# Where a loop begins in VectorE's instruction pages, a fetch hint on TensorE's loop, and one expert group a step later

## The chip, the core and the metric

One core of a Trainium2 chip runs the whole program; the other seven are idle. The metric is the device time of one execution in microseconds (us). The kernel before was timed three times: 2798.35, 2799.54 and 2804.08 us, median 2799.54 us.

A core has five engines that run their own instruction streams and meet at semaphores: TensorE (PE in the rows; its weight loads are PEld), VectorE (DVE), ScalarE (ACT), GpSimd (POOL) and the DMA-issuing SyncE (SP). DMA engines move the data, and the engines' own instructions too.

## The reference

Three layers act on an image batch x of 32 x 64 x 16 x 16, which is 8192 tokens of 64 values:

```
x = x + conv3x3(groupnorm(x), circulant mix of the weight)
t = t + attention over 80000 edges (segment sums per node, exp of clipped scores)
t = t + moe(layernorm(t)):
    h = (x @ W_gat).reshape(M, 4 heads, 4 experts)
    e = leaky_relu(a_src[src] + a_dst[dst]);  softmax of e over the edges of each dst
    agg = segment_sum(h[src] * alpha, dst) + b_gat
    scores = mean over heads of layernorm(agg);  top-2 of 4 experts, softmax of the two
    out = sum over experts of g_e * (gelu(x @ W1[e] + b1[e]) @ W2[e] + b2[e])
```

The third layer has 262144 edges, of which those whose target lies within the 8192 tokens count. The change lies in the edge loop of this layer and in the stage after it.

## The kernel before

All engines' programs are written out by hand, with waits on counting semaphores. The stages in time: sort the attention's edges and convolve (to about 450 us), attend in 20 chunks while the third layer's edges are sorted (to about 1300 us), lay out the gating tables and run the first 14 of 16 expert groups (to about 1800 us), the **gating loop** (to 2653 us), and the **finish** (gates, top 2, experts 56 to 63, output; to the end).

**The gating loop.** The sorted edges are cut into chunks of 128 rows by 64 edges. How many chunks there are depends on the data (`n_all`, here 17, at most 32), so every engine that takes part runs a real loop over `it`, each pass with two halves `b = 0, 1` for chunk `it * 2 + b`, each half inside an `If` on `n_all`. VectorE's loop goes over `it = 1..16`, TensorE's over 1..15. With 17 chunks, passes 1 to 7 do two chunks, pass 8 does chunk 16 and then the last sums, and all later passes find every `If` false: they run only compares and branches.

In a half, GpSimd fetches 36 of the 64 source rows of a chunk with one indirect DMA each; the other 28 ("picks") come from TensorE, in 7 batches: `spread` (4 small matmuls) puts 4 columns of keys on all partitions, ScalarE's `all_keys` casts them, VectorE's `one_hot` compares them with 8 columns of numbers, `pick` runs 96 matmuls with the one-hot matrices as weights, and VectorE's `take_picked` picks the candidate. `pick` of a batch needs its `one_hot`; `one_hot` of batch m needs the `pick` of batch m - 2 (its buffer). Between the batches VectorE does `flags`, `maximum` and `weighted_sums` of the chunk before.

VectorE's half has 104 + 28 + 7 + 11 + 11 instructions as built, then a compare and a block of 27 for the last sums (`it * 2 + b == n_all`). The whole loop is 385 instructions as built, 8 of them branches to the very next instruction, which fall away. From the loop's first instruction counted, its branch targets that an empty pass visits are at 0 (head), 160, 187, 347 and 375; the last instruction, the back edge, is at 376. TensorE's loop body has 1447 rows as built, of which 1400 are matmuls with a weight load each, so about 2840 instructions.

**The finish.** The nodes are gated in 3 pieces, each in 4 parts, in the order `FINISH_ORDER` = (0,0) (0,1) (0,2) (0,3) (1,0) (1,1) (1,2) (2,0) (1,3) ... A part on VectorE ends in a semaphore for a ScalarE function (exp, sqrt, exp) that the next part waits for. The last 8 expert units (two groups of four) are put between: ScalarE does their gelus before its parts 1 and 2, and VectorE adds the groups' results (`expert_group(14)`, `(15)`) before its parts at places 2 and 3. TensorE runs the units one after the other; unit n's second matmuls need its gelu.

Of the kernel before, what the change touches and what calls it, by code (L numbers as in the profile page):

```python
# [56 lines left out]
G_CHUNKS = G_W // G_RUN  # L57
# [123 lines left out]
def build(nc, io, debug=None):  # L181
    with ExitStack() as ctx:
# [120 lines left out]
        first = r.at  # L303
# [184 lines left out]
        HS_FIRST, HS_EACH = 16 * G_RUN, 16 * (G_RUN - PICKS)  # L488

        EXPERTS_FIRST, EXPERTS_EARLY = 10, 14  # L490

        block = ctx.enter_context(nc.Block())

        def bc(ap, shape):
            return ap.to_broadcast(shape)
# [303 lines left out]
        def _(pe):  # L799
# [189 lines left out]
            def spread(it, b, m):  # L989

                if m == 0:
                    pe.wait_ge(pick_keys_set, it * 2 + (b - 1))
                pe.wait_ge(pick_all_set, chunk_count(it, b, BATCHES, m + 1))
                for k in range(BATCH):
                    last = nc.tensor.matmul(ps[turn_of(b, m)][:, k * P:(k + 1) * P], bc(pick_key[b][:, BATCH * m + k:BATCH * m + k + 1], [P, P]), ident16,  # L995
                                            start=True, stop=True)
                last.then_inc(pick_spread, 1)

            def pick(it, b, m):
                pe.wait_ge(pick_hot_set, chunk_count(it, b, BATCHES, m + 3))  # L1000
                pe.wait_ge(pick_taken, chunk_count(it, b, BATCHES, m + 1))
                for k in range(BATCH):
                    for t in range(K_TILES):
                        for n in range(SPLITS):
                            last = nc.tensor.matmul(ps[2 + turn_of(b, m)][:, k * PICK_W:(k + 1) * PICK_W], pick_hot[turn_of(b, m)][:, t, k * P:(k + 1) * P],  # L1005
                                                    h_split[n][:, t * PICK_W:(t + 1) * PICK_W],
                                                    start=t == 0 and n == 0, stop=t == K_TILES - 1 and n == SPLITS - 1)
                last.then_inc(picked, 1)
# [6 lines left out]
            with pe.If(n_all >= 3):  # L1015
                for m in range(2):
                    spread(1, 0, m)
            with pe.Fori(1, G_CHUNKS // 2) as it:
                for b in range(2):
                    with pe.If(it * 2 + b < n_all):  # L1020
                        for m in range(BATCHES - 2):
                            spread(it, b, m + 2)
                            pick(it, b, m)
                        for m in range(2):
                            pick(it, b, BATCHES - 2 + m)
                            with pe.If(it * 2 + (b + 1) < n_all):
                                spread(it + b, 1 - b, m)
# [59 lines left out]
        def _(act):  # L1087
# [135 lines left out]
            def gelu(n):  # L1223
                act.wait_ge(hid_done, n + 1)
                if n >= 2:
                    act.wait_ge(hid_used, n - 1)
                nc.scalar.activation(hid[n % 2], ps[4 + n % 2][:, :], ACT.Gelu, bias=b1[:, n % 4:n % 4 + 1]).then_inc(hid_set, 1)  # L1227
# [41 lines left out]
            def lay_out(n):  # L1269
                for k in range(G_PIECES[n][0] // 4, G_PIECES[n][1] // 4):  # L1270
                    act.wait_ge(out_turned, k + 1)
                    nc.scalar.copy(out_ch[:, 2 * k:2 * k + 2, :].rearrange("p j s -> p (j s)"), ps[k % 2][:, :]).then_inc(out_laid, 1)

            for at_, (n, part) in enumerate(FINISH_ORDER):
                if at_ in (1, 2):
                    for unit in range(4 * EXPERTS_EARLY + 4 * at_ - 4, 4 * EXPERTS_EARLY + 4 * at_):
                        gelu(unit)
                at = slice(2 * G_PIECES[n][0], 2 * G_PIECES[n][1])
                if part == 0:
                    act.wait_ge(node_exp_in, n + 1)  # L1280
                    for k in range(3):
                        nc.scalar.activation(n4[4 + k][:, at], n4[4 + k][:, at], ACT.Exp).then_inc(node_exp, 1)
                elif part == 1:
                    act.wait_ge(gate_root_in, n + 1)
                    nc.scalar.activation(ln_var[:, at], ln_var[:, at], ACT.Sqrt).then_inc(gate_root, 1)
                elif part == 2:
                    act.wait_ge(gate_exp_in, n + 1)
                    nc.scalar.activation(n4[8][:, at], n4[8][:, at], ACT.Exp).then_inc(gate_exp, 1)
                elif n >= 1:
                    lay_out(n - 1)  # L1290
# [4 lines left out]
        def _(dve):  # L1295
# [17 lines left out]
            def tt(o, a_, b_, op):  # L1313
                return V.tensor_tensor(o, a_, b_, op)  # L1314
# [429 lines left out]
            def expert_group(grp):  # L1744
                dve.wait_ge(hid_used, 4 * grp + 4)
                i0 = grp % 8 * 4
                for k in range(2):
                    ins = tt(exp_tile[:, grp // 8, i0 + 2 * k:i0 + 2 * k + 2], ps[6 + k][:, :].rearrange("p (i e c) -> p i e c", e=4, c=CH),
                             bc(b2.rearrange("p (e c) -> p e c", c=CH)[:, None], [P, 2, 4, CH]), ALU.add)
                ins.then_inc(exp_taken, 1)  # L1750
# [22 lines left out]
            def flags(it, b, back):  # L1773
                g_done[0] = 0
                dve.wait_ge(g_idx_in[b], it * 48 + (48 - 48 * back * b))
                link(it, b, back, tt(g_nst.rearrange("p (h j) -> p h j", j=G_COLS)[:, :, 1:], bc(g_didx[b][:, None, :], [P, G_HEADS, G_RUN]),
                                     bc(g_dprev[b][:, None, :], [P, G_HEADS, G_RUN]), ALU.is_equal))
                ts(g_cut, g_nst, BIG, ALU.mult, -BIG, ALU.add).then_inc(g_flags, 1)
# [58 lines left out]
            def one_hot(it, b, m):  # L1837
                dve.wait_ge(pick_all_set, chunk_count(it, b, BATCHES, m + 3))
                dve.wait_ge(picked, chunk_count(it, b, BATCHES, m + 1))
                for t in range(K_TILES):  # L1840
                    ins = ts(pick_hot[turn_of(b, m)][:, t], pick_all[turn_of(b, m)], node[:, t:t + 1], ALU.is_equal)
                ins.then_inc(pick_hot_set, 1)
# [11 lines left out]
            def picked_a_src(it, b):  # L1854
                rows_ = hs[b][:, G_RUN - PICKS:]
                prod_ = pick_prod[:, 0:PICKS * G_HF]
                pick_link(it, b, tt(prod_.rearrange("p (j f) -> p j f", f=G_HF), rows_[:, :, 0:G_HF], bc(att[:, 0:1, :], [P, PICKS, G_HF]), ALU.mult))
                pick_link(it, b, V.tensor_reduce(rows_[:, :, G_HF:], prod_.rearrange("p (j h k) -> p j h k", h=G_HEADS, k=G_EXP), AX_X, ALU.add))
# [12 lines left out]
                one_hot(1, 0, 1)  # L1871

            with dve.Fori(1, G_CHUNKS // 2 + 1) as it:
                for b in range(2):
                    with dve.If(it * 2 + b < n_all):
                        p_done[0] = 0
                        flags(it, 1 - b, 1)
                        for m in range(BATCHES - 2):
                            one_hot(it, b, m + 2)  # L1880
                            take_picked(it, b, m)
                            if m == 1:
                                maximum(it, 1 - b, 1)
                            if m == 2:
                                weighted_sums(it, 1 - b, 1)
                        for m in range(2):
                            dve.sem_inc(waits_carried, 1)
                            with dve.If(it * 2 + (b + 1) < n_all):
                                if m == 0:
                                    pick_keys(it + b, 1 - b)  # L1890
                                one_hot(it + b, 1 - b, m)
                            take_picked(it, b, BATCHES - 2 + m)
                        picked_a_src(it, b)
                        dve.sem_inc(waits_carried, 1)
                        assert p_done[0] == PICK_STEPS
                    with dve.If(it * 2 + b == n_all):
                        flags(it, 1 - b, 1)
                        maximum(it, 1 - b, 1)
                        weighted_sums(it, 1 - b, 1)
                        V.tensor_copy(row_tail, g_didx[1 - b][:, G_RUN - 1:G_RUN])  # L1900
                        dve.sem_inc(waits_carried, 1)
# [135 lines left out]
            step(ts(g_nodes.seed_f, g_nodes.carried, BIG, ALU.mult, -BIG, ALU.add))  # L2037
            parts = [finish(n, 2 * lo, 2 * hi) for n, (lo, hi) in enumerate(G_PIECES)]
            for at_, (n, _) in enumerate(FINISH_ORDER):
                if at_ in (2, 3):  # L2040
                    expert_group(EXPERTS_EARLY + at_ - 2)
                next(parts[n])

# [36 lines left out]
```

## Time and profile before

| | us |
|---|---|
| median of 3 runs | 2799.54 |
| the profiled execution | 2800.3 |
| its span | 2798.2 |
| VectorE busy | 1984.4 (71%) |
| GpSimd busy | 1758.9 (63%) |
| TensorE matmul busy | 1213.3 (43%) |
| ScalarE busy | 538.6 (19%) |

The span runs from the first to the last instruction of the program; 2.1 us of the execution lie around it. "Issue" in the rows is time in which an engine waited for nothing that the profile shows. Compares, branches and register operations are not counted as busy. DMA queues of the kind "instruction" carry the engines' programs.

### The profile page before, as it was taken

The page shows a single profiled execution, that of the slowest core. Times are in us where ns is not written, and L with a number is a line of the kernel's source. Part 1 is how long each engine was busy: PE and PEld are TensorE (multiplying, and loading weights), DVE is VectorE, ACT ScalarE, POOL GpSimd, SP SyncE. Part 2 cuts the span into 40 slices and gives each one's busy share as a digit, 9 for nine tenths or more (in the row PEclk, how much of TensorE's full clock was granted, in tenths as well). Part 3 has the DMA queues.
Part 4 walks back from the last instruction along what each step waited for, and adds up shares of the span by engine and source line. Part 5 has one row for each costly group of instructions (what it writes and reads, how often), then busy time and mean ns, then how long its engine had stood idle before and what let it go on. Part 6 is the DMA issues. An engine that isn't in the chain of part 4 may idle for free.

```text
span 2798.2 us, 34080 instructions
## 1 busy us (share of the span) xinstructions
PE 1213.3 (43%) x12544; PEld 1018.1 (36%) x12544; DVE 1984.4 (71%) x3113; ACT 538.6 (19%) x639; POOL 1758.9 (63%) x1690
## 2 busy tenths in 40 slices
PE   4855000000001001010214595988888889784095
PEld 2432000000000000000203353688888879784075
DVE  7788776897787888788886301287888888885046
ACT  1011000222313223132101112122222222222011
POOL 0000577777777777773777677777777777773700
PEclk9976555555555555555555555598999999997558
DMA  9400211332323233232226234112221221211101
GB/s 297 172 0 0 78 46 65 112 101 96 113 81 112 90 107 114 82 114 64 50 82 55 70 120 80 9 24 39 25 38 25 25 38 25 39 25 29 14 2 31
DMA packets 145798, 188.12 MB, mean 67 GB/s; under 512 B 84844, under 2 KB 103982, under 8 KB 139166
## 3 DMA queue, kind: packets, MB, share of 16 engines
q1 hardware_dynamic: 91494, 121.72, 14.1%
q0 software_dynamic: 54080, 63.61, 12.4%
q8 instruction: 117, 1.92, 0.3%
q14 instruction: 107, 0.88, 0.1%
HBM read 97.32 MB, written 87.92 MB: 66 GB/s over the span
## 4 chain that ended last, share of the span: by engine, by line
POOL 32%; DVE 26%; PE 17%; issue 17%; DMA 3%; ACT 2%; SPq 2%; DVEq 0%; POOLq 0%; ACTq 0%
POOL arena L682 29%; DVE arena L1314 12%; PE psum L1005 9%; DVE arena L1317 6%; PE psum L888 2%; POOL d_adseed L769 2%; DVE arena L1803 2%; DVE arena L1852 2%; PE psum L966 2%; PE psum L978 2%; POOL d_qseed L706 1%; PE psum L1050 1%; DVE psum L1642 1%; ACT arena L1157 1%; DVE arena L1663 1%
## 5 line engine op out<-in xcount | busy, mean ns | idle before, releaser
L1314 DVE TENSOR_TENSOR arena<-arena 128x512 f32<-128x512 f32 (+17 forms) x1333 | 853.6, 680 | 261.6 <-issue 106.8
L682 POOL DMA_INDIRECT arena<-d_h,arena x668 | 692.5, 1037 | 211.2 <-issue 202.0
L682 POOL DMA_INDIRECT arena<-in_kv,arena x640 | 647.2, 1011 | 200.0 <-issue 193.6
L1005 PE MATMUL psum<-arena 128*128 128x128 bf16 x10080 | 621.0, 225 | 88.6 <-DVEq L1850 83.0
L1005 PEld LDWEIGHTS psum<-arena 128*128 128x128 bf16 x10080 | 606.3, 101 | 95.2 <-DVE arena L1317 84.8
L802 PE MATMUL psum<-arena 128*128 128x128 f32 (+3 forms) x444 | 100.5, 400 | 1191.7 <-DVEq L1391 1040.8
L802 PEld LDWEIGHTS psum<-arena 128*128 128x128 f32 (+3 forms) x444 | 79.4, 209 | 1214.0 <-DVEq L1391 1055.6
L1317 DVE TENSOR_SCALAR arena<-arena 128x512 bf16<-128x512 f16 (+9 forms) x1067 | 339.5, 376 | 79.4 <-ACT arena L1221 20.1
L1314 DVE TENSOR_TENSOR arena<-psum,arena 128x512 f32<-128x512 f32 (+2 forms) x179 | 167.2, 942 | 210.3 <-PE psum L966 202.4
L682 POOL DMA_INDIRECT arena<-d_adst,arena x40 | 54.4, 1361 | 305.7 <-DVEq L1488 293.8
L1642 DVE TENSOR_TENSOR_SCAN psum<-psum,arena 128x1024 f32<-128x1024 f32 x40 | 91.9, 2298 | 138.4 <-ACT arena L1144 137.5
L966 PEld LDWEIGHTS psum<-arena 128*128 128x128 f32 x512 | 113.7, 328 | 138.4 <-issue 100.5
L966 PE MATMUL psum<-arena 128*128 128x64 f32 x512 | 125.1, 427 | 46.5 <-ACT arena L1227 30.2
L978 PE MATMUL psum<-arena 64*128 64x512 f32 x128 | 131.3, 1132 | 0.6 <-ACT arena L1267 0.6
L1157 ACT COPY arena<-arena 128x2304 f32<-128x2304 f32 x20 | 88.0, 4398 | 197.2 <-DVEq L1665 197.2
L1221 ACT CAST arena<-psum 128x512 f16<-128x512 f32 x105 | 63.1, 602 | 314.1 <-PE psum L995 314.0
L1852 DVE TENSOR_REDUCE arena<-arena 128x64 f32<-128x512 f32 x105 | 106.5, 1014 | 15.7 <-DVE arena L1314 7.9
L1141 ACT COPY arena<-arena 128x1984 f32<-128x1984 f32 x20 | 73.3, 3665 | 186.2 <-DMA arena<-d_qseed 147.1
L682 POOL DMA_INDIRECT arena<-d_gs,arena x64 | 60.5, 946 | 58.8 <-SPq L665 39.5
L1663 DVE TENSOR_TENSOR_SCAN arena<-psum,arena 128x1024 f32<-128x1024 f32 x40 | 88.9, 2264 | 0.0
L1227 ACT ACTIVATE arena<-psum,arena 128x512 f32<-128x512 f32 x64 | 43.8, 688 | 234.2 <-PE psum L978 234.2
L682 POOL DMA_INDIRECT arena<-d_gdst,arena x64 | 75.4, 1178 | 20.8 <-issue 20.8
(183 smaller groups left out, 1379.7 us busy)
## 6 DMA issues: line engine op xcount, KB each, us to landing
d_gs<-arena SPq DMA_DIRECT2D x32, 768.0 KB, 12.2
d_as<-arena SPq DMA_DIRECT2D x20, 1152.0 KB, 4.5
d_qseed<-arena SPq DMA_DIRECT2D x5, 4096.0 KB, 29.4
arena<-d_qseed SPq DMA_DIRECT2D x20, 1024.0 KB, 5.8
arena<-d_h,arena POOLq DMA_INDIRECT x668
arena<-in_kv,arena POOLq DMA_INDIRECT x640
d_adseed<-arena SPq DMA_DIRECT2D x1, 4096.0 KB, 29.9
arena<-d_adseed SPq DMA_DIRECT2D x17, 128.0 KB
```

The source lines that it names most:

```text
L682: return pool.indirect_dma_start(out, None, table, bass.IndirectOffsetOnAxis(index[:, t:t + 1], 0))
L802: return nc.tensor.transpose(out, in_, ident[0:n, 0:n])
L966: last = nc.tensor.matmul(ps[6 + k // 2][:, k % 2 * 256 + e * CH:k % 2 * 256 + (e + 1) * CH], hid[n % 2][:, k * P:(k + 1) * P], w2[:, e, : ...
L978: nc.tensor.matmul(ps[4 + n % 2][:, :], w1[at, e, :], yT[at, i0:i0 + 4, :].rearrange("p i n -> p (i n)"), start=True, stop=True).then_inc( ...
L1005: last = nc.tensor.matmul(ps[2 + turn_of(b, m)][:, k * PICK_W:(k + 1) * PICK_W], pick_hot[turn_of(b, m)][:, t, k * P:(k + 1) * P], h_split ...
L1141: nc.scalar.copy(by_f[:, :, 1:], q_seed[b].rearrange("p j f -> p f j")[:, :, 1:])
L1157: nc.scalar.copy(a_rows[b].rearrange("p j f -> p f j"), a_sum.rearrange("p (f j) -> p f j", j=A_RUN)).then_inc(a_rows_set, 1)
L1314: return V.tensor_tensor(o, a_, b_, op)
L1317: return V.tensor_scalar(o, a_, s1, s2, op0, op1) if op1 is not None else V.tensor_scalar(o, a_, s1, None, op0)
L1642: step(V.tensor_tensor_scan(q_edge, a_go, q_fm[:, at], 0.0, ALU.mult, ALU.add))
L1663: last = V.tensor_tensor_scan(a_sum[:, at], a_go, a_msg[:, at], 0.0, ALU.mult, ALU.add)
L1852: pick_link(it, b, V.tensor_reduce(hs[b][:, lo:lo + BATCH, 0:G_HF], prod_.rearrange("p j k f -> p j f k"), AX_X, ALU.add))
```

## The change

The second late expert group moves from place 2 to place 3 of the finish (with its gelus, and VectorE's `expert_group(15)` from place 3 to place 4).

```diff
         EXPERTS_FIRST, EXPERTS_EARLY = 10, 14
+        LATE_EXPERTS = (1, 3)
...
-            with pe.Fori(1, G_CHUNKS // 2) as it:
+            with nc.Fori(1, G_CHUNKS // 2, engines=[mybir.EngineType.PE], hint_back_edge=True) as it:
...
             for at_, (n, part) in enumerate(FINISH_ORDER):
-                if at_ in (1, 2):
-                    for unit in range(4 * EXPERTS_EARLY + 4 * at_ - 4, 4 * EXPERTS_EARLY + 4 * at_):
+                if at_ in LATE_EXPERTS:
+                    first = 4 * (EXPERTS_EARLY + LATE_EXPERTS.index(at_))
+                    for unit in range(first, first + 4):
                         gelu(unit)
...
-            with dve.Fori(1, G_CHUNKS // 2 + 1) as it:
+            with nc.Fori(1, G_CHUNKS // 2 + 1, engines=[mybir.EngineType.DVE], head_slot={mybir.EngineType.DVE: 0}) as it:
...
             for at_, (n, _) in enumerate(FINISH_ORDER):
-                if at_ in (2, 3):
-                    expert_group(EXPERTS_EARLY + at_ - 2)
+                if at_ - 1 in LATE_EXPERTS:
+                    expert_group(EXPERTS_EARLY + LATE_EXPERTS.index(at_ - 1))
                 next(parts[n])
```

VectorE at the loop's entry, before (the last one-hots ahead of the loop, the entry, the head):

```order
L1317 TENSOR_SCALAR arena<-arena 128x512 x16
L1868 UNCONDITIONAL_BRANCH
L1874 UNCONDITIONAL_BRANCH
L1874 ISA
L1876 COMPARE_AND_BRANCH
```

and now, with lines two further down in the text:

```order
L1319 TENSOR_SCALAR arena<-arena 128x512 x16
L1870 UNCONDITIONAL_BRANCH
L1876 ISA
L1876 UNCONDITIONAL_BRANCH
L1876 ISA
L1878 COMPARE_AND_BRANCH
```

The first ISA row is the alignment; nothing inside the loop has moved.

ScalarE in the finish, before (L1227 is gelu, L1285 the sqrt of part 1, L1288 the exp of part 2, L1282 the exps of part 0):

```order
L1227 ACTIVATE arena<-psum,arena 128x512 x4
L1285 ACT_TABLE_LOAD
L1285 ACTIVATE arena<-arena 128x24
L1227 ACT_TABLE_LOAD
L1227 ACTIVATE arena<-psum,arena 128x512 x4
L1288 ACT_TABLE_LOAD
L1288 ACTIVATE arena<-arena 128x96
L1282 ACTIVATE arena<-arena 128x96 x3
```

and now:

```order
L1228 ACTIVATE arena<-psum,arena 128x512 x4
L1287 ACT_TABLE_LOAD
L1287 ACTIVATE arena<-arena 128x24
L1290 ACT_TABLE_LOAD
L1290 ACTIVATE arena<-arena 128x96
L1228 ACT_TABLE_LOAD
L1228 ACTIVATE arena<-psum,arena 128x512 x4
L1284 ACT_TABLE_LOAD
L1284 ACTIVATE arena<-arena 128x96 x3
```

The exp of part 2 stands ahead of the second four gelus, and there is one table load more.

VectorE in the finish, before (L2020 to L1314 end part 2 of piece 0, the psum row is `expert_group(15)`, L2025 begins part 3, whose end is the 4x1536 row; L1960 is in part 0 of piece 1):

```order
L2020 TENSOR_REDUCE arena<-arena 128x24
L1314 TENSOR_TENSOR arena<-arena 128x96
L1314 TENSOR_TENSOR arena<-psum,arena 128x2x4x64 x2
L2025 SCALAR_TENSOR_TENSOR arena<-arena 128x96
L2026 TENSOR_REDUCE arena<-arena 128x24
L2027 RECIPROCAL arena<-arena 128x24
L1314 TENSOR_TENSOR arena<-arena 128x96
L1314 TENSOR_TENSOR arena<-arena 128x4x1536
L1314 TENSOR_TENSOR arena<-arena 128x96
L1960 SCALAR_TENSOR_TENSOR arena<-arena 128x96
```

and now:

```order
L2022 TENSOR_REDUCE arena<-arena 128x24
L1316 TENSOR_TENSOR arena<-arena 128x96
L2027 SCALAR_TENSOR_TENSOR arena<-arena 128x96
L2028 TENSOR_REDUCE arena<-arena 128x24
L2029 RECIPROCAL arena<-arena 128x24
L1316 TENSOR_TENSOR arena<-arena 128x96
L1316 TENSOR_TENSOR arena<-arena 128x4x1536
L1316 TENSOR_TENSOR arena<-psum,arena 128x2x4x64 x2
L1316 TENSOR_TENSOR arena<-arena 128x96
L1962 SCALAR_TENSOR_TENSOR arena<-arena 128x96
```

The group's addition has moved past part 3 and stands ahead of piece 1. On TensorE one row is new, a BRANCH_PREFETCH_HINT at the loop's head.

## Rows read from the trace of the kernel before

**Rows 1.** The page, its first line.
```profile
span 2798.2 us, 34080 instructions
```

**Rows 2.** VectorE's timeline (start, us, engine, line, operation, [idle before <-releaser]), 2530 to 2700.
```profile
2574.69 0.15 DVE L1900 CAST arena<-arena 128x1 f32<-128x1 int32 x1
2653.31 0.55 DVE L1314 TENSOR_TENSOR arena<-arena 128x1 f32<-128x1 f32 x3 [78.47 <-issue]
```

**Rows 3.** The chain that ended last (start, us, what), 2520 to 2700.
```profile
2596.51 3.29 issue
2599.95 2.23 issue
```

**Rows 4.** The page's DMA queues (packets, MB, share of 16 engines).
```profile
q14 instruction: 107, 0.88, 0.1%
```

**Rows 5.** The DMA queues in the stretch 2590 to 2647.
```profile
q14 instruction: 30, 0.25, 1.7%
```

**Rows 6.** The DMA queues in the stretch 2414 to 2512, one full pass.
```profile
q8 instruction: 13, 0.21, 0.9%
q14 instruction: 5, 0.04, 0.1%
```

**Rows 7.** ScalarE's timeline, 2530 to 2700.
```profile
2574.63 3.37 ACT L1215 COPY arena<-arena 128x1280 f32<-128x1280 f32 x1 [5.43 <-DVEq L1804]
2583.72 1.28 ACT L1264 ACT_TABLE_LOAD   x1 [5.08 <-issue]
```

**Rows 8.** VectorE's timeline, 2398 to 2500: pass 7's head, then its second half.
```profile
2414.49 0.43 DVE L1314 TENSOR_TENSOR arena<-arena 128x256 f32<-128x256 int32 x1 [3.62 <-issue]
...
2420.02 2.54 DVE L1317 TENSOR_SCALAR arena<-arena 128x512 bf16<-128x512 f16 x8 [0.57 <-PE psum L1005]
...
2462.99 0.43 DVE L1314 TENSOR_TENSOR arena<-arena 128x256 f32<-128x256 int32 x1 [0.96 <-DVE arena L1858]
```

**Rows 9.** TensorE's timeline, 2398 to 2500, around its back edge.
```profile
2407.65 0.40 PE L995 MATMUL psum<-arena 128*128 128x128 f16 x4 [3.13 <-issue]
...
2410.26 4.14 PE L1005 MATMUL psum<-arena 128*128 128x128 bf16 x71 [0.81 <-issue]
...
2414.46 5.52 PE L1005 MATMUL psum<-arena 128*128 128x128 bf16 x96
```

**Rows 10.** VectorE's timeline, 2530 to 2700: pass 8's last sums.
```profile
2560.28 0.43 DVE L1314 TENSOR_TENSOR arena<-arena 128x256 f32<-128x256 int32 x1 [3.33 <-issue]
...
2563.27 0.70 DVE L1783 TENSOR_TENSOR_SCAN arena<-arena 128x260 f32<-128x260 f32 x1 [2.24 <-ACT arena L1197]
```

**Rows 11.** The page's groups (line, engine, operation, count | busy, mean ns | idle before).
```profile
L682 POOL DMA_INDIRECT arena<-d_h,arena x668 | 692.5, 1037 | 211.2 <-issue 202.0
```

**Rows 12.** GpSimd's waits, 1807.5 to 2548 (us in total, times, longest).
```profile
POOL arena L682 <- DMA arena<-d_gdrow: 9.2, 6, 3.1
```

**Rows 13.** GpSimd's timeline, 2530 to 2700.
```profile
2546.41 0.94 POOL L682 DMA_INDIRECT arena<-d_h,arena  x1 [0.30 <-issue]
2586.88 0.95 POOL L682 DMA_INDIRECT arena<-d_gs,arena  x1 [39.53 <-SPq L665]
```

**Rows 14.** VectorE's timeline, 2684 to 2800, the finish.
```profile
2694.29 3.80 DVE L1314 TENSOR_TENSOR arena<-arena 128x384 f32<-128x384 f32 x8 [5.45 <-ACT arena L1282]
...
2711.20 1.29 DVE L1314 TENSOR_TENSOR arena<-psum,arena 128x512 f32<-128x512 f32 x2 [8.06 <-PE psum L966]
...
2718.73 0.26 DVE L1314 TENSOR_TENSOR arena<-arena 128x96 f32<-128x96 f32 x1
2724.61 1.29 DVE L1314 TENSOR_TENSOR arena<-psum,arena 128x512 f32<-128x512 f32 x2 [5.63 <-PE psum L966]
...
2726.72 7.26 DVE L1314 TENSOR_TENSOR arena<-arena 128x96 f32<-128x96 f32 x3
```

**Rows 15.** ScalarE's timeline, 2684 to 2800, the finish.
```profile
2709.31 0.69 ACT L1227 ACTIVATE arena<-psum,arena 128x512 f32<-128x512 f32 x1 [0.38 <-PE psum L978]
...
2723.01 0.28 ACT L1288 ACTIVATE arena<-arena 128x96 f32<-128x96 f32 x1
```

## The prediction

> **What bounds the kernel now.** I read VectorE's timeline around the end of the gating loop first, because the change touches this loop. VectorE ends the last sums at 2574.84 (2574.69 + 0.15) and executes nothing for 78.47 us, waiting for "issue", that is for no other engine [rows 2]. This is passes 9 to 16, in which every `If` is false: GpSimd has done 668 gathers in this layer [rows 11], 64 + 64 for chunks 0 and 1 and 36 for each of 15 more, so there are 17 chunks and pass 8 is the last with work. The chain that ended last runs through this stall in pieces of about 3 us, for instance 3.29 and 2.23 [rows 3]. Eight empty passes in 78.47 us are 9.8 us each, for 8 branches and compares.
>
> What they wait for: the instruction queue q14 carries pages of 8 KB (0.88 MB in 107 packets) [rows 4]. In the six passes from 2590 to 2647 it moved 30 pages, 5 per pass [rows 5], and in a full pass 5 too [rows 6]. So per pass all five pages are fetched anew, although an empty pass uses 8 instructions of them. TensorE's loop needs 13 packets of 16 KB (0.21 MB) per pass [rows 6] for some 2840 instructions; the first and last page are only partly used, so 12 pages of 16 KB make about 240 instructions a page, which I take as 256, and 128 in one of 8 KB.
>
> ScalarE shows that an empty pass need not cost this: its loop has the same 16 passes, and between the start of its last big copy and the table load behind the loop lie 9.09 us, in which it ran through the same 8 empty passes [rows 7]: at most 1.14 us each, hidden beside two copies.
>
> The rest of the loop is shared. At VectorE's back edge there are 3.62 us without work, against 0.96 where pass 7 goes on from its first half to its second: 2.66 for the jump [rows 8]. TensorE stands 3.13 us at its own back edge and 0.81 more at the next page [rows 9]. GpSimd is nearly always busy: of 740 us it waited 9.2 for indices [rows 12].
>
> **VectorE's loop at a page's first slot.** Its 377 instructions then lie in pages 0, 1 and 2 (slots 0 to 376, the third page ends at 383), and the page fetched ahead is the fourth. Before, five pages per pass means four of the body and one ahead. So the question is whether an engine with 8 KB pages keeps four. From below: ScalarE's loop has some 113 instructions, which 7 placings in 8 put on two pages; with the page ahead it uses three, and yet all 5 packets per pass are VectorE's own count (four of the body, one ahead) [rows 6], so ScalarE refetched none and keeps at least three. From above: five are too many, or VectorE would not refetch. So it keeps three or four, and I take four, because TensorE, too, jumps among far pages in its empty passes without a packet (no q8 in [rows 5]). [...]
>
> With four kept, nothing is fetched after the first pass:
> - Empty passes: 8 x 1.2 = 9.6 us (ScalarE's 1.14, a little more for VectorE) in place of 78.5: -68.9. They are all on the path: behind them come the tail sums, which every later one-hot and the finish need.
> - The jump of pass 8 over its second half to the last sums: 3.33 us of issue [rows 10] become about 0.5: -2.8.
> - Back edges between full passes, 7 of them: -2.66 each on VectorE alone, if TensorE lets it.
> - The entry: at most one missed page, 2.9 us, which lies beside 3 us of one-hots still queued: 0.
>
> **TensorE's hint.** If the head's page is there in time, 3.13 becomes about 0.3 (my estimate for a taken jump to a page that is there: ScalarE's empty pass has eight jumps in 1.14), and the 0.81 stays, since the second page is asked for only from the head: -2.5 to -2.8 per pass on TensorE. What of it counts: after the head VectorE's next one-hots wait for TensorE's first two picks. Before, one_hot(2) followed VectorE's first operation without a wait, at about 2415, with pick(0) done at 2414.40 (2410.26 + 4.14) and one_hot(3) at 2420.02, when pick(1) was done (2414.46 + 5.52), after 0.57 of waiting [rows 8, 9]. So the two engines arrive together. VectorE's edit alone gains nothing here (pick(1) still ends at 2419.98), the hint alone 0.57, both together the smaller of 2.66 and 2.5. That is 7 x 2.5 = 17.5 us. The hint's own instruction, once a pass, is under 0.2 us on an engine that waits elsewhere: 0.
>
> **What becomes late next.** GpSimd gathers 36 rows a chunk at 1.04 + 0.31 (202.0 us of issue over 668) = 1.35 us each [rows 11]: 48.6. Its last gather for the loop ends at 2547.35 [rows 13]; without the 9.2 us of waits for indices, most of which vanish when VectorE frees them earlier, it ends at about 2540, and lands some 2.4 us later. VectorE's maximum of chunk 16, which needs these rows, began at 2563.27 [rows 10] and would be at 2563.27 - 17.5 - 2.8 = 2543.0. So GpSimd is just not late: the loop's gain is 20.3 us, and it cannot be much over 21. Its gathers for the finish start when the last rows are stored, at 2586.88 [rows 13], so 20.3 earlier too, at 2566.6; the first 24 need 24 x 1.25 (0.95 + 0.30 [rows 13]) = 30 us plus landing: 2599. VectorE arrives there about 89 us earlier than before, at 2597; it had 5.45 us of waiting for ScalarE right behind [rows 14], which hide the 2 us. The other 40 rows come in time.
>
> **The late expert group.** Before, VectorE waited 8.06 us for group 14 and 5.63 for group 15, whose sums began at 2724.61; part 3 followed and ended at 2733.98 (2726.72 + 7.26) [rows 14]. Now ScalarE's exp of part 2 is ahead of the last four gelus. It waits for VectorE's part 2, which ends at 2718.99 [rows 14], so the exp runs at 2719.1 instead of 2723.01, and the gelu that ran at 2709.31 [rows 15] is at 2719.4 + 1.28 (table load) = 2720.7, done at 2721.4. TensorE stands meanwhile, from about 2713.2. From 2711.20 to 2724.61 it had done 7 pieces, 1.92 each; after that gelu 6 are left: 2721.4 + 11.5 = 2732.9. Part 3 on VectorE: 2719.4 to 2727.3. Then group 15 at 2732.9 + 1.3, and piece 1 begins at 2734.2, where it began at 2734.0. The wait of 5.6 us has moved behind part 3: +0.2 to +0.6, I take +0.5. The added table load hides in it.
>
> **The sum**, against the profiled execution, 2800.3 (span 2798.2 [rows 1] and 2.1 around it): 2800.3 - 68.9 - 2.8 - 17.5 + 0.5 = 2711.6. The profiled execution is 0.8 above the median, so 2711.
>
> **Rivals.**
> - *The hint does not reach the page in time.* VectorE waits at one_hot(3) as before and its seven back edges gain nothing: 2799.5 - 68.9 - 2.8 + 0.5 = 2728. For it: the hint stands at the head, some 2840 instructions ahead of its jump, and 12 pages pass in between. Against: nothing in the trace, no hint is in it.
> - *An engine keeps only the page it is in and the next.* Then every back edge misses as before, and only the jump to 347 goes from a miss into a page under way: -1 us in each empty pass (a piece of 2.23 for one of 3.29 [rows 3]), the whole 2.8 in pass 8, and 0.57 x 7 by the hint: 2799.5 - 8 - 2.8 - 4 + 0.5 = 2785. Three pages give the same. [...] ScalarE's loop without packets [rows 6, 7] speaks against two.
> - *The slot is not kept* (the loop's body lies over four pages as now): 2796 to 2800, by the hint alone.
> - *Slower: the hint's fetch pushes out a page that the picks are about to need.* Place: TensorE's page crossings in pass 1 to 8, 12 a pass. Price: 3.13 each [rows 9]. Against a gain of 71.7 it decides from three such misses a pass (8 x 3 x 3.13 = 75); at four it is 2799.5 - 71.7 + 100 = 2828. For it only that TensorE's body has more pages than fit; against it, that a page lasts some 7 us and a fetch 3.
>
> **How the numbers follow.** Forecast 0.62; late hint 0.17; two or three pages 0.12; slot not kept 0.05; slower 0.03; 0.01 for something else that is faster. The forecast's own range is 2704 to 2722: below, empty passes of 0.9 us and GpSimd's bound; above, five of the seven back edges given back to waits on keys and picks. With the late hint's case the range is 2702 to 2738, about 0.8. A measurement of this kernel can tell about 0.2% (5.6 us) from no change. Faster by more than that: 0.62 + 0.17 + 0.12 + 0.01 + a little of the slot's case = 0.93; same 0.04; slower 0.03.
>
> **What would show it.** Right: between the CAST of L1902 and the next row of VectorE some 9 to 11 us in place of 78.47; in this stretch no q14 packets of VectorE, and one full pass with none or one; full passes of 96 us instead of 99; idle before VectorE's flags at the head about 1 us, before TensorE's spread under 0.6; GpSimd's gathers of the loop ending near 2540; the wait for group 15 now ahead of piece 1, 5 to 6 us long. Wrong: 25 us or more in the empty passes with packets in them (fewer pages kept), TensorE still at 3 us (hint late), or one_hot(3) waiting for more than 1 us (TensorE bounds the head).

## The result, and the profile after

| | before | after |
|---|---|---|
| median, us | 2798.94 (4 runs) | 2710.41 (4 runs, 2708.72 to 2710.84) |
| profiled execution | 2800.3 | 2710.24 |
| its span | 2798.2 | 2708.4 |

The ratio is 0.9682, with a 95% interval of 0.9665 to 0.97. The forecast was 2711. (A fourth run of the kernel before moved its median from 2799.54 to 2798.94.)

Five sections of the span, cut at rows of VectorE, add up to the difference of 89.8 us:

| section | before | after | difference | forecast |
|---|---|---|---|---|
| start to the loop's first flags | 1809.63 | 1805.02 | -4.6 | 0 |
| from there to the end of the last sums (2574.84 and 2550.68) | 765.21 | 745.66 | -19.6 | -20.3 |
| end of the last sums to the tail | 78.47 | 11.33 | -67.1 | -68.9 |
| tail to piece 1 of the finish | 80.70 | 81.23 | +0.5 | +0.5 |
| piece 1 to the end | 64.19 | 65.16 | +1.0 | 0 |

The first section holds no edit. In the ten kernels that were profiled on chips of this speed the loop's first flags start between 1802.83 and 1809.63 us, and the profile of the kernel before is the latest of them. So 4.6 us of the difference between the two profiles are a difference between executions, and no gain of the change. The second section is not exact to the us either: the kernel before with a computed loop end, told below, whose loop does the same work up to there, takes 762.1 us for it. The entry to VectorE's loop lies here too: the branch that is new there starts at 1801.51, the loop's first register operation at 1804.70, 3.2 us later, and a q14 packet starts between them (1802.85). Before, that operation followed the one ahead of it within 0.1 us (1805.99, 1806.07). VectorE's one-hots run on beside the jump, up to the flags, so the 0 that the forecast took for the entry held. The two first flags, before and after:

```profile
1809.63 0.41 DVE L1314 TENSOR_TENSOR arena<-arena 128x256 f32<-128x256 int32 x1
```

```profile
1805.02 0.41 DVE L1316 TENSOR_TENSOR arena<-arena 128x256 f32<-128x256 int32 x1
```

VectorE's timeline after (start, us, engine, line, operation, [idle before <-releaser]), 2380 to 2565: pass 7's head, the last sums, the empty passes. It answers to [rows 2, 8, 10].

```profile
2383.91 0.42 DVE L1316 TENSOR_TENSOR arena<-arena 128x256 f32<-128x256 int32 x1 [0.97 <-DVE arena L1860]
...
2539.12 0.70 DVE L1785 TENSOR_TENSOR_SCAN arena<-arena 128x260 f32<-128x260 f32 x1 [11.73 <-ACT arena L1198]
...
2545.08 2.28 DVE L1316 TENSOR_TENSOR arena<-arena 128x1024 f32<-128x1024 f32 x1 [2.08 <-ACT arena L1208]
...
2550.53 0.15 DVE L1902 CAST arena<-arena 128x1 f32<-128x1 int32 x1
2562.01 0.55 DVE L1316 TENSOR_TENSOR arena<-arena 128x1 f32<-128x1 f32 x3 [11.32 <-issue]
```

The idle time ahead of the head's flags was 3.62 with "issue"; now it is 0.97, and its releaser is VectorE's own last reduction, as in the middle of a pass. The 78.47 became 11.32: eight empty passes of 1.4 us. New is a wait of 11.73 in the last chunk, before its maximum.

The page's DMA queues after, for the whole span (packets, MB, share of 16 engines); [rows 4] showed 107 for q14, and q8 had 117 before:

```profile
q8 instruction: 110, 1.80, 0.3%
q14 instruction: 34, 0.28, 0.0%
```

The DMA queues from 1906 to 2479, six full passes; [rows 6] showed 13 and 5 for one pass:

```profile
q0 software_dynamic: 13440, 4.33, 15.0%
q1 hardware_dynamic: 8640, 12.19, 5.9%
q8 instruction: 72, 1.18, 0.8%
```

There is no q14 line: in 573 us not one of its pages of 8 KB was fetched, where it had been 30 in the six full passes of the kernel before (1915 to 2513). q8, whose packets are of 16 KB and follow TensorE's jumps (below), still carries pages anew in every pass, but 12 where it was 13: 72 packets in six full passes, against 78.

TensorE's timeline around its back edge, 2368 to 2400, which answers to [rows 9]:

```profile
2370.82 5.52 PE L1006 MATMUL psum<-arena 128*128 128x128 bf16 x96
2376.18 0.66 PE L996 MATMUL psum<-arena 128*128 128x128 f16 x8
2376.67 1.50 PE L1006 MATMUL psum<-arena 128*128 128x128 bf16 x24
2379.07 4.18 PE L1006 MATMUL psum<-arena 128*128 128x128 bf16 x72 [0.89 <-issue]
```

The 3.13 us at the jump are gone so completely that the last spread of one pass and the first of the next form one group of eight. The 0.89 at the second page stays. The trace of TensorE's branches and of q8's packets shows what the hint did. Before, the back edge's branch took 3.34 to 3.72 us at the seven jumps behind passes 1 to 7; one packet started 3.8 to 5.7 us ahead of it, a second 0.9 to 1.1 us into it, a third 4.1 to 4.5 us behind its start. Now it takes 0.35 to 0.40 us; one packet starts 3.9 to 5.9 us ahead of it, none in it, and the next 1.0 to 1.7 us behind its start. So the head's page was fetched inside the jump and is now there ahead of it, and one packet a pass is gone. The next one still starts only behind the head.

The chain that ended last, 2480 to 2708, at the last chunk (start, us, what):

```profile
2535.08 0.94 POOL arena L683
2536.33 2.54 DMA arena<-d_h,arena
2539.12 0.71 DVE arena L1785
```

Before, the chain ran through TensorE's picks and VectorE's one-hots here. Now 41% of the chain over the whole span is GpSimd's gathers (29% before). From 1900 to 2500 they are 53% of it and the "issue" time, most of it between gathers, another 19%. GpSimd's waits for indices from 1803 to 2538 (us, times, longest), which answer to [rows 12], are nearly gone, so that it gathers without a stop:

```profile
POOL arena L683 <- DMA arena<-d_gdrow: 0.6, 2, 0.3
```

The finish on VectorE, 2590 to 2660, answers to [rows 14]:

```profile
2619.91 1.29 DVE L1316 TENSOR_TENSOR arena<-psum,arena 128x512 f32<-128x512 f32 x2 [8.03 <-PE psum L967]
...
2628.16 0.26 DVE L2027 SCALAR_TENSOR_TENSOR arena<-arena 128x96 f32<-128x96 f32 x1 [0.41 <-ACT arena L1290]
...
2641.75 1.29 DVE L1316 TENSOR_TENSOR arena<-psum,arena 128x512 f32<-128x512 f32 x2 [5.82 <-PE psum L967]
2642.96 0.25 DVE L1316 TENSOR_TENSOR arena<-arena 128x96 f32<-128x96 f32 x1
2643.24 0.26 DVE L1962 SCALAR_TENSOR_TENSOR arena<-arena 128x96 f32<-128x96 f32 x1
```

The wait for group 15 is 5.82 where it was 5.63, and stands behind part 3; ScalarE's exp now lets VectorE wait 0.41.

### The profile page after: what moved, and what is told of

Read it like the earlier page. It is cut to its first block, busy times and chain, and to the rows that moved or that the text cites. A ratio compares the mean times of both kernels' runs of the same rounds, so it can differ in the third digit from the quotient of the medians.

```text
span 2708.4 us, 34097 instructions
## 1 busy us (share of the span) xinstructions
PE 1207.7 (45%) x12544; PEld 1013.0 (37%) x12544; DVE 1985.4 (73%) x3113; ACT 540.9 (20%) x640; POOL 1764.9 (65%) x1690
## 4 chain that ended last, share of the span: by engine, by line
POOL 45%; DVE 20%; issue 17%; PE 12%; DMA 3%; ACT 2%; SPq 1%; DVEq 0%; POOLq 0%; ACTq 0%
POOL arena L683 41%; DVE arena L1316 13%; DVE arena L1319 3%; PE psum L1006 3%; PE psum L889 2%; POOL d_adseed L770 2%; PE psum L967 2%; PE psum L979 2%; POOL d_qseed L707 1%; PE psum L1051 1%; PE psum L803 1%; DVE arena L1805 1%; SPq L523 1%; DVE arena L1854 1%; DMA arena<-d_gdrow 1%
## 5 line engine op out<-in xcount | busy, mean ns | idle before, releaser
L1006 PE MATMUL psum<-arena 128*128 128x128 bf16 x10080 | 611.2, 224 | 93.4 <-DVEq L1852 84.2
L1006 PEld LDWEIGHTS psum<-arena 128*128 128x128 bf16 x10080 | 597.0, 100 | 98.8 <-DVE arena L1319 88.0
L1854 DVE TENSOR_REDUCE arena<-arena 128x64 f32<-128x512 f32 x105 | 106.5, 1015 | 15.7 <-DVE arena L1316 8.2
L683 POOL DMA_INDIRECT arena<-d_gs,arena x64 | 67.2, 1049 | 42.4 <-SPq L666 23.2
L1316 DVE TENSOR_TENSOR arena<-arena,psum 128x2048 f32<-128x2048 f32 (+3 forms) x31 | 78.3, 2527 | 14.1 <-PE psum L858 12.6
```

Source lines behind the costliest of these rows:

```text
L683: return pool.indirect_dma_start(out, None, table, bass.IndirectOffsetOnAxis(index[:, t:t + 1], 0))
L1854: pick_link(it, b, V.tensor_reduce(hs[b][:, lo:lo + BATCH, 0:G_HF], prod_.rearrange("p j k f -> p j f k"), AX_X, ALU.add))
```

## The experiments

The theory had three claims: VectorE's side keeps four pages of 128 instructions; the back edges gain only where both engines lose their miss; and after the change GpSimd's gathers are the bound of the loop. Ten kernels tested them, two of them on two chips. Four ran on a chip on which the kernel before took 3751.56 us (20 runs) instead of 2799; they are told last, and their times are not compared with the others. The rest ran on two chips on which the kernel before took 2796.37 us (13 runs: slots 7 and 8, the changed kernel without empty passes, fewer gathers) and 2798.67 (11 runs: the others). Each ratio is against the kernel before on the same chip.

### One edit at a time

VectorE's slot alone:

```diff
-            with dve.Fori(1, G_CHUNKS // 2 + 1) as it:
+            with nc.Fori(1, G_CHUNKS // 2 + 1, engines=[mybir.EngineType.DVE], head_slot={mybir.EngineType.DVE: 0}) as it:
```

> Only VectorE's loop begins at slot 0 of a page; TensorE's loop has no hint, the late groups stand as before. Theory 1 (the back edges gain only where both engines lose their miss): 67 us of empty passes and 2.9 of pass 8's jump go, the seven back edges give 0 to 4 in all, as TensorE still stands 3.1 at its own: 2723 to 2728 us where the kernel before takes 2798, full passes of 99 to 99.6 us. Theory 2 (VectorE's miss alone sets the pass): 2.66 x 7 = 18.6 more off, to GpSimd's bound: 2709 to 2712, full passes under 97.

Measured: 2725.22 us, ratio 0.9736 (0.9723 to 0.9749).

TensorE's hint alone:

```diff
-            with pe.Fori(1, G_CHUNKS // 2) as it:
+            with nc.Fori(1, G_CHUNKS // 2, engines=[mybir.EngineType.PE], hint_back_edge=True) as it:
```

> Only TensorE's back edge is hinted. Theory 1: TensorE's 3.1 us go, VectorE's 2.7 to 3 stay, and only its waits for picks go, at most 1.5 us a full pass: 2788 to 2796 us where the kernel before takes 2798, full passes of 98 to 99.3 us. Theory 2 (TensorE's miss alone sets the pass): 3.1 x 7 = 22 off: 2776 to 2780.

Measured: 2791.29 us, ratio 0.9976 (0.9965 to 0.9987).

The two edits part the instruction queues: with the slot alone q14 moves 33 packets in the span where it was 107, and q8 its 117 as before; with the hint alone q8 moves 110 and q14 108.

Both times lie where theory 1 put them, and the two alone make 73.4 + 7.4 = 80.8 us (against 2798.67), while the whole change makes 88.5. The other 8 exist only together. As a difference of whole times that is only just beyond the three intervals (about 5, 4 and 3 us) taken together; the lengths of the passes, below, are the clearer evidence. The waits of VectorE in the six full passes (us in total, times, longest) show the mechanism. Before, 1915.2 to 2512.9:

```profile
DVE arena L1314 <- issue: 21.5, 6, 3.7
...
DVE arena L1317 <- PE psum L1005: 9.0, 8, 1.5
```

The slot alone, 1907.4 to 2504.7:

```profile
DVE arena L1317 <- PE psum L1005: 24.7, 12, 4.9
```

The hint alone, 1911.2 to 2503.6:

```profile
DVE arena L1314 <- issue: 21.8, 6, 3.8
```

With the slot alone the 21.5 us of "issue" are gone, 3.7 of them return as waits for VectorE's own reduction (5.8 to 9.5), and the waits for picks grow from 9.0 to 24.7: nearly all the rest, 15.7, comes back as a wait for TensorE, which still stands at its back edge. Full passes take (2504.72 - 1907.44) / 6 = 99.5 us, as before (99.6). With the hint alone the waits for picks vanish from the list and the 21.8 stay: 98.7 us. With both, both are gone: (2479.47 - 1906.22) / 6 = 95.5. (The heads' times are those of the loop's first register operation.) So a back edge was worth 2.7 us of missing page plus 1.5 of waiting for picks: of the 4.1 us a pass that both edits bring, the slot alone brings 0.1 and the hint alone 0.9.

### How many pages

```diff
-            ... head_slot={mybir.EngineType.DVE: 0}) as it:
+            ... head_slot={mybir.EngineType.DVE: 7}) as it:
```

and the same with 8.

> The whole change with VectorE's loop head at slot 7 in place of slot 0: its 377 instructions end at slot 383, the last of the third page. Theory 1 (what counts is how many pages of 128 instructions the body touches, and four are kept): the same as with slot 0, 2710 us on a chip where the kernel before takes 2799, no instruction packets for VectorE from pass 2 on, 11 us between the last sums and the tail. Rival (the head itself must stand at a page's start, so that it is fetched with its successor): some of the gain goes, 2715 to 2780.

> The whole change with VectorE's loop head at slot 8: one instruction, the back edge, now lies in a fourth page (slot 384). Theory 1 (four pages are kept; entering the fourth asks for the fifth, which takes the place of a page of the body): every pass fetches again, 5 packets of 8 KB each, the empty passes cost nearly the 78 us of before and the back edge misses: 2785 to 2796 us where the kernel before takes 2799, 80 us more for one slot. Rival 1 (five or more pages fit): 2710 as with slot 0, and no packets. Rival 2 (only the fifth and one more are refetched, the others stay): 2 to 4 packets a pass, 2730 to 2770.

Measured: slot 7 2710.63 us (2709.86 to 2712.32; ratio 0.9694, 0.9678 to 0.971), slot 8 2802.1 us (2800.38 to 2806.06; ratio 1.0017, 1.0007 to 1.0026). One slot costs 91.5 us. The page of slot 7:

```profile
q14 instruction: 35, 0.28, 0.0%
```

The page of slot 8, and VectorE's row behind its empty passes:

```profile
q14 instruction: 109, 0.89, 0.1%
```

```profile
2657.45 0.55 DVE L1316 TENSOR_TENSOR arena<-arena 128x1 f32<-128x1 f32 x3 [91.05 <-issue]
```

Slot 8 puts only the back edge into a fourth page, and q14 moves 30 pages in the six full passes (1911 to 2507) again, 5 a pass: four of the body and a fifth asked for on entering the fourth. Three of the five start at the back edge (2007.40, 2007.81 and 2011.18, where the branch starts at 2006.65 and the head's first register operation at 2010.23), the others in the pass (2047.32, 2073.81). Theory 1 of slot 8 holds in its mechanism, but the time lies 6 us above its range: the empty passes cost 91 us, more than the 78.5 of before. In an empty pass VectorE now also stands 2.1 us ahead of the back edge itself, between the loop's register operation (start 2588.72) and the compare in the fourth page (2590.86), and then 3.5 us for the jump back. TensorE's hint was in this kernel; it could not make up for it.

### A hint on VectorE's loop instead

```diff
-            ... engines=[mybir.EngineType.DVE], head_slot={mybir.EngineType.DVE: 0}) as it:
+            ... engines=[mybir.EngineType.DVE], hint_back_edge=True) as it:
```

> The whole change with a hint on VectorE's back edge in place of its slot, so its body lies over four pages again. Theory 1: in full passes the page of the head is there in time, as on TensorE, and the loop's gain of about 24 us comes as in the whole change; in the empty passes the jumps inside the body still miss, 5 packets a pass, and the hint saves at most the back edge's 3 us of each: 2752 to 2776 us where the kernel before takes 2798. Rival (with the hint the pages settle and are kept): 2710. Rival 2 (the hint does nothing where pages are short): 2790 to 2796.

Measured: 2717.61 us, ratio 0.9709 (0.9694 to 0.9724), the rival's side. My theory of the hint fell here. The page's queue and VectorE's timeline behind the empty passes:

```profile
q14 instruction: 33, 0.27, 0.0%
```

```profile
2547.66 0.15 DVE L1902 CAST arena<-arena 128x1 f32<-128x1 int32 x1
2564.23 0.55 DVE L1316 TENSOR_TENSOR arena<-arena 128x1 f32<-128x1 f32 x3 [16.42 <-issue]
```

The body lies over four pages as before, and yet nothing is fetched after pass 1. In pass 1 of the kernel before, four packets of q14 start 10.3, 24.5, 58.6 and 96.0 us behind the head; in this one three, at 10.2, 24.3 and 58.5. The fourth is missing. It started 10.2 us ahead of the back edge's branch (1902.10, 1912.26); I read it as the page behind the loop, asked for on entering the body's last page. The next packet of q14 starts only at 2601.4 us, 37 us behind the loop. So with a hint on the back edge the page behind the loop was not asked for, and a body of four pages stayed whole. (TensorE's hint also brought one packet of q8 a pass less, 110 in the span against 117, in the hint alone too.) This is the strongest evidence that four pages are kept: four pages of body with a fifth asked for lose all, four without it lose nothing.

An empty pass costs 2.03 us here against 1.4 with the slot. The hint itself is 0.08 of that; the rest lies at the four compares of the two halves, each of which takes 0.12 to 0.13 us in place of 0.06, with a longer gap behind it. Why stays open. The empty passes put this kernel 5.1 us behind the slot's (16.42 against 11.32); the last sums end 2.9 us earlier (2547.81 against 2550.68). The profiled executions differ by 2.5 us and the medians by 7.2; the profiled one was the fastest of its four, and no profile shows the cause of the rest.

### No empty passes

```diff
-            with dve.Fori(1, G_CHUNKS // 2 + 1) as it:
+            with dve.Fori(1, n_all // 2 + 1) as it:
```

on the kernel before, and on the changed one (with its slot).

> The kernel before with nothing changed but the end of VectorE's loop, which is computed from the number of chunks: no slot, no hint, late groups as before. If what the slot brings is in the main the empty passes: the 78.5 us between the last sums and the tail become 1 to 4 and some 3 us of new waits come behind them (for the stored rows): 2723 to 2728 us, with the back edges of full passes missing as before (passes of 99.6 us). Rival (pages that are missed elsewhere, outside the empty passes, are part of the 70 us): 2740 to 2760.

> The whole change with VectorE's loop ending at a bound computed from the number of chunks (8 passes here in place of 16), so that it runs no empty pass. Theory 1: the empty passes that are left cost 1.4 us each and all on the path: the 11.3 us between the last sums and the tail become 1 to 3: 9 us less than the whole change, 2701 where that takes 2710. Rival: the tail then waits for the other engines (TensorE's and ScalarE's loops, or stored rows): 0 to 5 less.

Measured: on the kernel before 2724.03 us (2717.73 to 2726.73), ratio 0.9735 (0.972 to 0.975); on the changed one 2705.43 (2703.87 to 2707.69), ratio 0.9676 (0.966 to 0.9692). The first is as fast as the slot alone (2725.22): what the slot brings by itself is in the main the empty passes. (The two are not the same sum: this one loses all 78.3 us of them, but waits 5.05 us for the rows to be stored.) In the second, where the rival was nearly right and theory 1 expected 9, 11.32 us of empty passes bought only 5.2 (against slot 7 on the same chip, whose runs all lie above it). Its timeline on VectorE, 2550 to 2600, says where the rest went:

```profile
2562.19 1.41 DVE L1319 TENSOR_SCALAR arena<-psum,arena 128x512 f32<-128x512 f32 x2 [6.95 <-SPq L662]
...
2594.04 2.35 DVE L1316 TENSOR_TENSOR arena<-arena 128x96 f32<-128x96 f32 x9 [2.97 <-DMA arena<-d_gs,arena]
```

VectorE now waits 6.95 us for the last rows to be stored and 2.97 for GpSimd's gathers of them; the wait for ScalarE that follows shrinks from 5.43 to 2.50. The last of the cost lay beside other work already. This is the fastest of the kernels that compute everything.

### GpSimd as the bound

```diff
-        HS_FIRST, HS_EACH = 16 * G_RUN, 16 * (G_RUN - PICKS)
+        HS_FIRST, HS_EACH = 16 * G_RUN, 16 * (G_RUN - PICKS - 2)
...
-                        g_gather(b, G_RUN - PICKS)
+                        g_gather(b, G_RUN - PICKS - 2)
```

> The whole change, but GpSimd leaves out 2 of the 36 gathers of each chunk in the loop (those rows keep what was there), so a chunk costs it 46 us in place of 48.6. Theory 1 (after the change GpSimd's gathers are what the last chunk waits for: VectorE and TensorE reach it 9 to 14 us before the rows land): 9 to 14 us less than the whole change, 2697 to 2701 where that takes 2710, and VectorE's wait of 11.7 us before the maximum of chunk 16 is gone. Rival (the picks' chain of TensorE and VectorE is still the bound, the wait only a gap that something else fills): 0 to 3 us less.

Measured: 2696.64 us (2693.5 to 2697.57), ratio 0.9646 (0.963 to 0.9662), 14.0 below slot 7 on the same chip. VectorE's row of chunk 16's maximum:

```profile
2523.09 0.70 DVE L1785 TENSOR_TENSOR_SCAN arena<-arena 128x260 f32<-128x260 f32 x1 [2.24 <-ACT arena L1198]
```

The wait of 11.73 is back to the 2.24 of the kernel before [rows 10]. The full passes are no shorter than in the changed kernel ((2476.20 - 1903.32) / 6 = 95.5): VectorE and TensorE set the pass. In the changed kernel GpSimd takes 98.0 us for two chunks (chunk 2's first gather starts at 1803.25, chunk 16's at 2489.24, 14 chunks of 49.0), so it loses 2.5 us a pass, and its lead is used up only in the last chunk. It has not been tried how far the loop would go with a faster GpSimd and fewer waits on the other two.

### The late group, and the runs on the other chip

> Only VectorE's loop begins at slot 0 of a page; TensorE's loop has no hint, the late expert groups stand as before. Theory 1 (mine: a gain at the back edges between full passes needs both engines): the eight empty passes lose 67 us and pass 8's jump 2.9, the seven back edges nothing, since VectorE then waits for TensorE's picks right behind the head: 2799 - 70 = 2729 us, with VectorE's idle before the flags at the head about 1 us and its wait for picks in the pass grown by 2 to 3 us. Theory 2 (VectorE alone bounds the pass): its 2.66 x 7 = 18.6 us come off too: 2710. If an engine kept only three pages it would be 2785, which the run of the whole change has already spoken against.

> Only TensorE's back edge is hinted; VectorE's loop lies as before, the late expert groups too. Theory 1: TensorE's 3.1 us at its back edge go, but VectorE still misses the page of its head, so only the wait for picks behind the head goes, 0.57 to 1.5 us a pass: 2799 - 4 to - 10 = 2789 to 2795 us, and the 78 us of empty passes stay. Theory 2 (TensorE bounds the pass): 3.1 x 7 = 22 us off: 2777. No effect (the hint alone does not fetch the page): 2799.

> Only the second late expert group comes a step later; both loops as before. Theory 1: the wait of 5.6 us moves behind part 3 and grows by 0.2 to 0.6: 2799.5 us, no difference that can be measured; piece 1 begins 0.5 later. Rival: TensorE's stand while the gelus wait pushes out the whole finish by the added table load and the exp, 1.6 to 4 us: 2801 to 2803.

```diff
-                if at_ in (1, 2):
+                if at_ in LATE_EXPERTS:
...
-                if at_ in (2, 3):
+                if at_ - 1 in LATE_EXPERTS:
```

> Both loop edits, the second late expert group as before. Theory 1: the whole change without its 0.5 us in the finish: 2709.9 us. Rival: the later group is worth some us once GpSimd's last gathers are the bound (the finish waits for something else then), so this is slower than the whole change, 2712 to 2715.

```diff
-        LATE_EXPERTS = (1, 3)
+        LATE_EXPERTS = (1, 2)
```

Measured, against 3751.56 us on that chip: slot alone 3734.63, ratio 0.9956 (0.994 to 0.9972); hint alone 3752.71, 0.9996 (0.9984 to 1.0008); late group alone 3753.37, 1.0006 (0.9992 to 1.002); both loop edits 3719.61, 0.9916 (0.9892 to 0.9941). The slot alone brought 17 us where 70 were expected, the hint alone nothing that can be told. For the loops these runs decide nothing, since TensorE bounds the loop there (below); why both edits together bring 15 us more than the slot alone was not looked into. The slot's 67 us of empty passes did go (11.32 of issue behind them, as on the other chips), but VectorE then stood 10.4, 25.9 and 32.9 us ahead of three operations of the tail that read TensorE's results. The late group alone cannot be told from no change, as theory 1 has it. The run of both loop edits cannot be judged by its theories, since the whole change did not run on that chip.

The late group can be read all the same, because the stretch from group 14's sums to piece 1 has the same length on both chips. It is 22.81 us in the kernel before (2711.20 to 2734.01) [rows 14], in the slot alone and in the hint alone, and 22.81 also in the kernel with both loop edits on the other chip. It is 23.33 in the changed kernel (2619.91 to 2643.24), in slot 7 and in the hint on VectorE, and 23.27 with the late group alone (3667.74 to 3691.01). So the later group costs 0.5 us, below what the whole time can show.

## Why the prediction was right

**The empty passes: right.** -68.9 was forecast, -67.1 came. An empty pass costs VectorE 1.4 us instead of the 1.2 that I took from ScalarE's row [rows 7]. Four pages kept is shown by slot 7 against 8 (35 and 109 packets of q14) and by the hint on VectorE (33).

**Back edges: the mechanism right, the size too small, and the bound set elsewhere.** That the two edits need each other is shown by the two alone. But I took a gain of 2.5 us a pass, the smaller of the two engines' losses at the head, and it was 4.1 (99.6 to 95.5), since VectorE's other waits for picks in the pass (9.0 us in six passes, against the one of 0.57 that I had read) went too. From the loop's first flags to pass 8's head the kernel gained 28.9 us (703.3 to 674.45), seven times 4.1.

**What becomes late next: the engine right, the amount wrong.** I wrote that GpSimd "is just not late". It was late: 11.73 us of waiting in chunk 16, and the run with fewer gathers shows that these rows were what it waited for. That the loop's gain of 19.6 us lies so near the 20.3 of the forecast is therefore in part luck. Two errors cancelled: the back edges brought 28.9 in place of 17.5, and the wait for GpSimd's last gathers took most of the difference back. My bound, that the gain "cannot be much over 21", held, though its own terms were off. GpSimd's waits for indices fell from 9.2 to 0.6 us, but from chunk 2's first gather (1807.87 before, 1803.25 now) to the end of the last one (2547.35, 2537.27) it was only 5.5 us faster; the other 4.6 by which it ended earlier lie ahead of the loop, as in the table.

**Pass 8's jump**: it was 3.33 before [rows 10] and no longer shows; since the gathers come last there it was worth nothing of its own.

**The late group: right,** 0.52 for 0.5.

**The whole time: closer than its terms.** The forecast of 2711.6 was built on one profiled execution, and 2710.24 came. The 4.6 us ahead of the loop, which no term held, made up for 1.8 us too much in the empty passes, 0.7 too much in the loop and the last 1.0 us. That last one has no part in the change either: from piece 1 to the end the kernels took between 64.1 and 65.7 us, with and without the later group.

**A row that did not show what I read in it.** For four pages I took that TensorE jumps through its own empty passes without a packet, by [rows 5]. But that stretch begins at 2590 us, and TensorE's empty passes ran from 2561.6 to 2569.6. The fact is right (no q8 packet starts between 2562.2 and 2655.5), the row does not show it.

**The rivals.** "The hint does not reach the page in time" fell to TensorE's back edge; two or three pages, and the slot not kept, to the missing q14 line. "The hint's fetch pushes out a page" fell to the 12 q8 packets a pass. Jumps over three pages of 8 KB, and with the hint on VectorE over four, ran without a packet of q14 after pass 1.

## What to carry to other kernels

Count the pages that a loop's body touches before touching the loop: here a body of 377 instructions fetches nothing after pass 1 in three pages, and takes 91 us more over its 16 passes, 8 of them empty, when its last instruction slips into a fourth. Look in the profile for "issue" idle at a loop's head and for a steady number of instruction packets a pass, also where the loop's passes are empty. Where two engines miss at their back edges in the same pass, repair both (of the 4.1 us a pass one edit alone brought 0.1, the other 0.9), and look at once which engine is nearly saturated beside them: here GpSimd, for whose gathers VectorE then waited 11.73 us in the last chunk.

## What the runs showed of the hardware

- A hint on the back edge did more than fetch the head: with it the page behind the loop's last one was no longer asked for, so that a body of four pages stayed resident (33 packets of q14 in the whole span against 107). On TensorE, whose body does not stay, it saved one page a pass (72 packets of q8 in six passes against 78), and the jump took 0.35 to 0.40 us in place of 3.34 to 3.72.
- The same kernel took 3751.56 us on one chip and 2796 to 2799 on three groups of runs elsewhere. On the slow one TensorE stood for some 50 us in the last picks of each half of a pass, without a wait that the profile shows. Its timeline there (slot alone, 2790 to 2890):

```profile
2862.30 0.27 PE L1005 MATMUL psum<-arena 128*128 128x128 bf16 x1 [2.53 <-issue]
2864.40 0.26 PE L1005 MATMUL psum<-arena 128*128 128x128 bf16 x1 [1.84 <-issue]
2867.20 0.26 PE L1005 MATMUL psum<-arena 128*128 128x128 bf16 x1 [2.54 <-issue]
2870.00 0.26 PE L1005 MATMUL psum<-arena 128*128 128x128 bf16 x1 [2.54 <-issue]
```

  The matmuls start 2.1 or 2.8 us apart, multiples of 0.7, and none lasts longer than elsewhere (median of this line's matmuls 218 ns in both profiles); VectorE's operations last as on the other chip (1333 of line L1314, 680 ns in the mean on both). What holds TensorE back is open. It shows that a gain must be measured on the chip on which its base was measured: there the slot brought 17 us, here 73.
